# Window attention: the row maximum is taken off the scores by TensorE in PSUM instead of by VectorE

## The reference

```python
qkv = win @ w_qkv + b_qkv                        # win: (256 windows, 49, 32)
q, k, v = heads(qkv)                             # 4 heads, 8 channels each
attn = jnp.einsum('whnd,whmd->whnm', q, k) * scale
attn = jax.nn.softmax(attn, axis=-1)             # over the 49 keys m
out = jnp.einsum('whnm,whmd->whnd', attn, v)
out = out @ w_proj + b_proj
```

## Time and profile before

| | us |
|---|---|
| median of 3 runs | 478.54 |
| lowest, highest | 476.59, 478.87 |
| profiled execution | 475.85 |
| its span | 474.1 |
| VectorE busy in the span | 365.1 |
| TensorE matmul busy | 351.1 |
| ScalarE busy | 299.8 |
| GpSimd busy | 233.9 |
| first and last row-maximum reduction (start) | 31.8 and 141.6 |

### The profile page before, as it was taken

One profiled execution on the slowest core, in us unless ns is written; L12 is line 12 of the kernel. 1 busy time (PEld: TensorE's weight loads), 2 busy tenths in 40 slices (PEclk: granted clock), 3 DMA queues, 4 the chain that ended last, 5 costly groups with the idle time before them and its releaser, 6 DMA issues. The chain is left out here.

```text
span 474.1 us, 10021 instructions
## 1 busy us (share of the span) xinstructions
PE 351.1 (74%) x3480; PEld 230.4 (49%) x3480; DVE 365.1 (77%) x679; ACT 299.8 (63%) x583; POOL 233.9 (49%) x217
## 2 busy tenths in 40 slices
PE   5149888896789785985877647666795829888885
PEld 4037676675665332142233213222483519877774
DVE  3799999999797388799787999997576685544443
ACT  4327788887785899578758946347985253333432
POOL 4526868775673324966972999567081130000000
PEclk9997999998899999599897885768999668999999
DMA  6110000000223231022000000000030000111111
GB/s 147 5 18 3 3 1 0 0 1 0 59 60 70 51 87 29 1 60 58 1 0 1 0 1 0 0 0 1 3 68 3 1 0 11 20 19 22 22 19 24
DMA packets 24044, 10.29 MB, mean 22 GB/s; under 512 B 20576, under 2 KB 22368, under 8 KB 24016
## 3 DMA queue, kind: packets, MB, share of 16 engines
q1 hardware_dynamic: 23888, 9.93, 10.3%
q0 software_dynamic: 128, 0.01, 0.2%
HBM read 2.00 MB, written 1.61 MB: 8 GB/s over the span
## 5 line engine op out<-in xcount | busy, mean ns | idle before, releaser
L480 POOL TENSOR_TENSOR Pr<-Pr,rc 128x392 f32<-128x392 f32 x64 | 54.4, 883 | 32.2 <-DVE rc L1826 32.2
L511 POOL TENSOR_TENSOR YA<-YA,hC 128x784 f32<-128x784 f32 x27 | 51.7, 1914 | 32.4 <-DVE hC L1910 31.5
L1349 PE MATMUL pair<-BCf,sel 96*128 96x392 bf16 x128 | 38.4, 394 | 35.0 <-DVE Hs L1894 30.8
L1894 DVE TENSOR_TENSOR_SCAN Hs<-dA,pair 128x784 f32<-128x784 f32 x32 | 57.1, 1785 | 1.0
L1193 PE MATMUL pair<-ident,Pr 128*128 128x128 f32 x256 | 41.1, 293 | 13.2 <-ACT PT L715 9.0
L1349 PEld LDWEIGHTS pair<-BCf,sel 96*128 96x128 bf16 x128 | 10.2, 105 | 74.0 <-issue 71.6
L1193 PEld LDWEIGHTS pair<-ident,Pr 128*128 128x128 f32 x256 | 29.2, 146 | 25.1 <-ACT PT L715 15.8
L1887 DVE TENSOR_TENSOR pair<-DU,pair 128x784 f32<-128x784 f32 x32 | 31.1, 973 | 10.6 <-PE pair L1349 10.3
L715 ACT ACTIVATE PT<-pair 128x392 f32<-128x392 f32 x64 | 31.4, 497 | 5.9 <-PE pair L1193 5.6
L724 ACT ACTIVATE Pr<-Ts 128x392 f32<-128x392 f32 x64 | 32.5, 536 | 3.4 <-DVE Ts L1810 3.4
L1804 DVE TENSOR_REDUCE mx<-pair 128x8 f32<-128x392 f32 x64 | 32.6, 550 | 1.6 <-PE pair L1150 1.4
(11 more groups left out here) (262 smaller groups left out, 928.8 us busy)
## 6 DMA issues: line engine op xcount, KB each, us to landing
SX<-XP SPq DMA_DIRECT2D x48, 112.2 KB
XT<-in_x SPq DMA_DIRECT2D x4, 392.0 KB, 5.0
out<-Os SPq DMA_DIRECT2D x28, 56.0 KB, 1.8
AD<-Aa SPq DMA_DIRECT2D x4, 196.0 KB
NB<-in_L_conv_x_proj_w SPq DMA_DIRECT2D x4, 3.0 KB
DW<-in_L_conv_dw SPq DMA_DIRECT2D x4, 1.1 KB
vec<-in_L_conv_b_qkv POOLq DMA_DIRECT2D x3, 0.5 KB, 5.8
W<-in_L_conv_w_qkv SPq DMA_DIRECT2D x1, 48.0 KB
```

The lines of the kernel that those rows point to most:

```text
L480: eng.tensor_tensor(pg, pg, bcast(rc[:, g, :], 2, WT), ALU.mult).then_inc(pn_r, 1)
L511: eng.tensor_tensor(y, y, hC[:, n % NHC, :], ALU.add).then_inc(g_ya, 1)
L1349: ins = eng.matmul(SPREAD[s][:, columns(h)], sel[:, n, :], upper(BCf[:, c % 2, s, columns(h)]), start=True, stop=True)
L1894: eng.tensor_tensor_scan(Hs[:, n % 2, :], dA[:, n % NA, :], SPREAD[0], 0.0, ALU.mult, ALU.add).then_inc(v_s, 1)
```

## The change

The maximum is no longer subtracted by VectorE. For two groups at a time (a part), VectorE writes the 16 maxima of a partition as two bfloat16 pieces, an upper one (L1848) and the remainder (L1852), into `MP`. TensorE turns them against the identity into 32 rows of bank 7 (`turn_max`, L1175 of the changed kernel), and VectorE copies these to SBUF as `MT` in bfloat16 (L1857). TensorE then adds minus the maximum to the scores in their banks, with a matmul against a constant pattern `msel` (`shift`, L1183). The exponent reads PSUM. GpSimd sets `MT`, `mrow` and `msel` up at the start. `scores` now waits for the exponentials of the step before where it had waited for its subtractions. ScalarE's order changes too.

```diff
@@ TensorE, pe_att
-                        eng.wait_ge(sub_r, 4 * s - 2 + 2 * part)
+                        eng.wait_ge(exp_r, 4 * s - 2 + 2 * part)
...
-                                                 start=True, stop=True)
+                                                 start=pair == 0, stop=False, skip_group_check=True)
...
+                def turn_max(part):
+                    if not cur:
+                        return
+                    eng.wait_ge(max_r, 10 * s + (5, 8)[part])
+                    if part == 0 and (not fixed or s >= 2):
+                        eng.wait_ge(ao_r, s - 1)
+                    eng.matmul(shift_rows(part), MP[:, part, :], upper(ident[:, 0:QP]), start=True, stop=True,
+                               skip_group_check=True).then_inc(mt_r, 1)
+
+                def shift(part):
+                    if not cur:
+                        return
+                    eng.wait_ge(max_r, 10 * s + 9 + part)
+                    for g in (2 * part, 2 * part + 1):
+                        eng.matmul(banks[g][:, 0:392], MT[:, part, :], msel[:, g % 2].rearrange("p m k -> p (m k)"),
+                                   start=False, stop=True, skip_group_check=True).then_inc(sh_r, 1)
...
                 if prv:
                     transposes(0)
                     transposes(1)
+                turn_max(0)
                 if early:
                     early()
                 if prv:
                     transposes(2)
+                shift(0)
+                turn_max(1)
+                if prv:
                     transposes(3)
+                shift(1)
                 if prv2:
                     project()
@@ ScalarE, act_att
-                    eng.activation(Pr[:, par, g, :, 0:WT], Ts[:, g, :, :], ACT.Exp).then_inc(exp_r, 1)
+                    eng.activation(Pr[:, par, g, :, 0:WT], banks[g][:, 0:392].rearrange("p (m k) -> p m k", k=WT), ACT.Exp).then_inc(exp_r, 1)
 
                 turned_out(0)
+                turned_out(1)
+                turned_out(2)
                 exponent(0)
-                turned_out(1)
+                turned_out(3)
                 exponent(1)
-                turned_out(2)
-                turned_out(3)
                 exponent(2)
                 exponent(3)
@@ VectorE, dve_att
-                        for g in groups:
-                            eng.wait_ge(max_r, 4 * s + g + 1)
-                            if not fixed or s >= 1:
-                                eng.wait_ge(exp_r, 4 * (s - 1) + g + 1)
-                            eng.tensor_tensor(Ts[:, g, :, :], banks[g][:, 0:392].rearrange("p (m k) -> p m k", k=WT),
-                                              bcast(mx[:, g, :], 2, WT), ALU.subtract).then_inc(sub_r, 1)
...
+                    def upper_piece(part):
+                        eng.wait_ge(max_r, 10 * s + (2, 6)[part])
+                        if not fixed or s >= 1:
+                            eng.wait_ge(mt_r, 2 * s - 1 + part)
+                        eng.tensor_copy(MP[:, part, 0:16], mx[:, 2 * part:2 * part + 2, :].rearrange("p g m -> p (g m)")).then_inc(max_r, 1)
+
+                    def lower_piece(part):
+                        eng.wait_ge(max_r, 10 * s + (3, 7)[part])
+                        eng.tensor_tensor(MP[:, part, 16:32], mx[:, 2 * part:2 * part + 2, :].rearrange("p g m -> p (g m)"),
+                                          MP[:, part, 0:16], ALU.subtract).then_inc(max_r, 1)
+
+                    def turned_max(part):
+                        eng.wait_ge(mt_r, 2 * s + part + 1)
+                        eng.tensor_copy(MT[:, part, 0:QP], shift_rows(part)).then_inc(max_r, 1)
```

More of the change, by code:

```diff
@@ L113, in build @@
         Vst = sb("Vst", [P, 2, 2, NW // 2, G, 2, C], att)
-        Ts = sb("Ts", [P, G, 8, WT], att)
+        MP = sb("MP", [P, 2, 32], att, BF16)
+        MT = sb("MT", [32, 2, P], att, BF16)
+        mrow = sb("mrow", [32, 16], att)
+        msel = sb("msel", [32, 2, 8, WT], att, BF16)
         Pr = sb("Pr", [P, 2, G, 8, WP], att)
@@ L210, in build @@
         qk_d, v_r, s_r, t_r, av_r, pj_r, q_r, k_r, exp_r, ring_r = sems("qk_d v_r s_r t_r av_r pj_r q_r k_r exp_r ring_r")
-        xw_r, km_r, pn_r, max_r, sub_r, sum_r, rec_r, ao_r, x1_r = sems("xw_r km_r pn_r max_r sub_r sum_r rec_r ao_r x1_r")
+        xw_r, km_r, pn_r, max_r, mt_r, sh_r, sum_r, rec_r, ao_r, x1_r = sems("xw_r km_r pn_r max_r mt_r sh_r sum_r rec_r ao_r x1_r")
         PRODUCTS = "conv x2 u z delta xB xC out var wout".split()
@@ L236, in build, with shift_rows @@
         block = ctx.enter_context(nc.Block())
+        QP = 64 + WT
+        def shift_rows(part):
+            return banks[7][0:32, 256 + P * part:256 + P * part + QP]
         def strip(s):
@@ L457, in _ @@
                 eng.memset(m[:], 0.0).then_inc(s_mk2, 1)
+            eng.memset(MT[:], 0.0).then_inc(s_mk2, 1)
+            eng.wait_ge(s_mk, 5)
+            eng.tensor_tensor(mrow[:, :], ident[0:32, 0:16], ident[0:32, 16:32], ALU.add).then_inc(s_mk2, 1)
+            eng.wait_ge(s_mk2, 6)
+            eng.tensor_scalar(msel[:, :, :, :].rearrange("p g m k -> p (g m) k"), bcast(mrow[:, :], 2, WT), -1.0, None, ALU.mult).then_inc(s_mk2, 1)
             eng.wait_ge(s_mk2, 1)
@@ L720, in exponent @@
                         return
-                    eng.wait_ge(sub_r, 4 * s + g + 1)
+                    eng.wait_ge(sh_r, 4 * s + g + 1)
                     if not fixed or s >= 2:
                         eng.wait_ge(t_r, 4 * (s - 2) + g + 1)
-                    eng.activation(Pr[:, par, g, :, 0:WT], Ts[:, g, :, :], ACT.Exp).then_inc(exp_r, 1)
+                    eng.activation(Pr[:, par, g, :, 0:WT], banks[g][:, 0:392].rearrange("p (m k) -> p m k", k=WT), ACT.Exp).then_inc(exp_r, 1)
                 turned_out(0)
+                turned_out(1)
+                turned_out(2)
                 exponent(0)
-                turned_out(1)
+                turned_out(3)
                 exponent(1)
-                turned_out(2)
-                turned_out(3)
                 exponent(2)
@@ L1198, in av @@
                     eng.wait_ge(ring_r, base + G)
+                    if cur:
+                        eng.wait_ge(max_r, 10 * s + 10)
                     if not fixed or s >= 2:
@@ L1241, in _ @@
             pe_att(-1, 1)
+            eng.wait_ge(s_mk2, 7)
             for s in (0, 1, 2):
@@ L1283, in conv @@
                 if b == 0 and h == 0:
-                    eng.wait_ge(sub_r, 4 * NS - 2)
+                    eng.wait_ge(exp_r, 4 * NS - 2)
                 for y in taps:
@@ L1308, in delta @@
                 if b == 0:
-                    eng.wait_ge(sub_r, 4 * NS)
+                    eng.wait_ge(exp_r, 4 * NS)
                 eng.matmul(result("delta", b)[:, h, :], BD[:, U_DL, :], US[:, b, HT * h:HT * h + HT], start=True, stop=True).then_inc(p_["delta"], 1)
@@ L1799, in dve_att, with largest @@
                 if cur:
-                    for part in range(2):
-                        groups = (2 * part, 2 * part + 1)
-                        eng.wait_ge(s_r, 2 * s + part + 1)
-                        for g in groups:
-                            eng.tensor_reduce(mx[:, g, :], banks[g][:, 0:392].rearrange("p (m k) -> p m k", k=WT), AX.X,
-                                              ALU.max).then_inc(max_r, 1)
-                        for g in groups:
-                            eng.wait_ge(max_r, 4 * s + g + 1)
-                            if not fixed or s >= 1:
-                                eng.wait_ge(exp_r, 4 * (s - 1) + g + 1)
-                            eng.tensor_tensor(Ts[:, g, :, :], banks[g][:, 0:392].rearrange("p (m k) -> p m k", k=WT),
-                                              bcast(mx[:, g, :], 2, WT), ALU.subtract).then_inc(sub_r, 1)
+                    def largest(g):
+                        if g % 2 == 0:
+                            eng.wait_ge(s_r, 2 * s + g // 2 + 1)
+                        eng.tensor_reduce(mx[:, g, :], banks[g][:, 0:392].rearrange("p (m k) -> p m k", k=WT), AX.X,
+                                          ALU.max).then_inc(max_r, 1)
@@ new lines, in turned_max @@
+                    def turned_max(part):
+                        eng.wait_ge(mt_r, 2 * s + part + 1)
+                        eng.tensor_copy(MT[:, part, 0:QP], shift_rows(part)).then_inc(max_r, 1)
+                    largest(0)
+                    largest(1)
+                    upper_piece(0)
+                    largest(2)
+                    lower_piece(0)
+                    largest(3)
+                    upper_piece(1)
+                    lower_piece(1)
+                    turned_max(0)
@@ L1812, in dve_att @@
+                    turned_max(1)
                 if prv2:
```

## The result

The changed kernel takes 530.31 us (median of 5 runs, 529.92 to 534.85), the kernel before in the same comparison 476.59 (470.71 to 478.87). The ratio is 1.1215, with a 95% interval of 1.1116 to 1.1313. The sign of the forecast was right, but the size was not: +54 us where it said +16, and the time lies outside its range. The profiled execution took 534.85 us with a span of 533.1, against 475.85 and 474.1 before, so the differences of the two traces add up to 59.

The account below looks back on a forecast made before the run. VectorE's instruction list was taken to bound each attention step; 16 steps at +1.0 us, less 0.5 us, took 475.85 to 491.3, put at 492.5 us for the median of runs. Range 480 to 505, the forecast's own 487 to 501.

Parts of the forecast that it names:

- What bounds the kernel: Attention steps, 60 to 105 us: a step is as long as VectorE's list, 6.67 us; TensorE has some 0.7 us of room.
- What the change takes from VectorE: Four subtractions a step at 0.48 us spacing, 1.9 us; after added work and dependence gaps VectorE gains 0.85 us.
- What it adds to VectorE: Four 16-element pieces and two 113-element copies a step: 0.7 us of work, bounds 0.4 and 1.5, plus three gaps of 0.12.
- +8: Upper end of the range over 16 steps if VectorE's small instructions cost their upper bound, 0.5 us a step more.
- What it adds to TensorE: Two turnings and four shifts a step, 0.84 us, in a queue which had 0.7 us of room.
- The waits: VectorE waits 0.74 us before the second MT copy and 1.15 before the residual; step 7.6 us, taken as +1.0.
- What costs nothing: Exponentials reading PSUM cost ScalarE nothing; GpSimd's set-up falls into its 2.61 us wait, uncovered 0 to 2 us once.
- 0.5 us off for ScalarE's order: Stretch from 105 to 127 us: ring copies no longer stand behind exponentials, 0 to -3 us, taken as -0.5.
- VectorE's queue alone decides: TensorE answers in time, step 6.3 us, time 470 to 472, or 455 by the skill's prices; chance 0.09.
- Balance: Waits are served earlier as TensorE works ahead: +0.1 to +0.4 us a step, 477 to 483 us; chance 0.12.
- The clock rival: TensorE falls to its lower clock more often, some 1.8 us a step in half the steps: +14, 506 us; chance 0.12.
- a sign of being wrong: The forecast is wrong if the granted clock from 60 to 105 us isn't 1.00.

Follow-up runs that it names:

- the rebuilt kernel: Changed kernel with row maxima in PSUM and a new order on VectorE, TensorE (projection ahead of last shifts) and ScalarE: 488.81 us, 1.0278 of the kernel before.

## Why the prediction was wrong in size

**What bounds the kernel: right.** VectorE's list set the step: it was busy for 43.47 of 45 us, and cutting TensorE's work in the kernel before left the time where it was.

**What the change takes from VectorE: nearly.** With the maxima in PSUM, no piece held up, VectorE's busy time in the whole trace falls from 365.1 to 353.9 us, 0.7 us a step, where the forecast had 0.85 less work. From the first maximum to the first `MT` copy it is 2.74 us (71.85 to 74.59), laid out as 2.60.

**What it adds to VectorE: the step that failed.** I wrote "For 16 elements I take 0.17 long and 0.09 apart", with an upper bound of "each as long as the reciprocal's 0.25". Alone a piece does last 0.17. Measured in place it is 0.53 in the mean and 1.39 at most, because it stands still while GpSimd works. The nearest rows were small instructions without GpSimd beside them, and the reciprocal, which has it beside it, isn't stopped by it: all 32 stay within 240 and 254 ns after. I chose neighbours by size and not by where operands lie. That term was worth 31 of the 54 us: 23 inside the pieces, and 8 in what hangs on them. For TensorE waits for the pieces, its granted clock falls to 0.77, and its answers come later: VectorE's idle time from the first maximum to the last is 51.6 us in the changed kernel and 42.7 with the maxima in PSUM. The range of the sum had +8 for it.

**What it adds to TensorE: nearly.** A shift lasts 335 ns as priced (336), and a turning 225. But a pair of shifts takes 0.43 us of the queue and not 0.34, a turning 0.16 and not 0.08, and the quartet of transposes behind it 0.59 and not 0.53. TensorE's timeline, maxima in PSUM:

```profile
74.90 0.50 PE L1183 MATMUL pair<-msel,MT 32*128 32x392 bf16 x2 [0.25 <-DVE MT L1857]
75.33 0.23 PE L1175 MATMUL pair<-ident,MP 128*32 128x113 bf16 x1
75.49 0.66 PE L1223 MATMUL pair<-ident,Pr 128*128 128x128 f32 x4
76.08 0.50 PE L1183 MATMUL pair<-msel,MT 32*128 32x392 bf16 x2
76.51 0.60 PE L1205 MATMUL pair<-AO,BD 128*128 128x196 f32 x2
```

**The waits: right in place, a little small.** From the second turning's start to the projection's it is 1.18 us (75.33 to 76.51) where I laid out 0.95, and from there to the residual 0.77 instead of 0.64. These 0.36 us give the 0.27 between 1.42 and 1.15: I counted a copy's slot as 0.18, and the profile counts its whole 0.27 as work. The first upper piece starts 1.17 us after its first maximum (73.02 against 71.85) where I had 1.06, the first pair of shifts takes its 0.09 more ahead of the second turning, and the loop's branch leaves 0.56 us ahead of the maxima instead of 0.40, every other step. 7.6 + 0.36 + 0.11 + 0.09 + 0.08 is 8.24, and 8.0 to 8.4 was measured. The first ten of the 15 spacings of steps lose 1.45 us each (8.14 against 6.69), not 1.0. The last five, with the statistics and the table loads, lose 1.8 each (9.95 against 8.11). There I had taken 0.5 us off for ScalarE's order, and its gain in the kernel before isn't seen here; why isn't shown.

**What costs nothing: right.** The exponentials from PSUM have a median of 507 ns, where those from SBUF had a mean of 538. Set-up on GpSimd leaves the first maximum at 31.8 us, and the `MT` copies last 264 (0.28 forecast).

**The rivals.** That VectorE's queue alone decides was wrong, in the rebuilt kernel too, since TensorE takes over. Balance, at 477 to 483 us, didn't come either. The clock rival saw the fall (1.00 to 0.77), which the forecast had named as a sign of being wrong, and priced it at 14 us, where the runs leave 4.5 to 11. The fall follows from TensorE's waits for the pieces: with the maxima in PSUM the clock is 0.96. It isn't the main loss.

**The sum of +54:** 31 for the wait for GpSimd and the clock that falls with it, 9 to 12 for the residual behind the projection, and the remaining 11 to 14 for TensorE's added matmuls and the chain through the turnings. How this last part splits wasn't separated. The forecast's +16 was for the last two parts together, which measure 22; for the first it had nothing but the +8 of its range.

## What to carry to other kernels

Before a small instruction is priced by its size, look where its operands lie and what GpSimd does at that time: on VectorE, a cast of 16 elements from SBUF and a subtraction with two SBUF sources each took up to 1.4 us, nearly the whole of a GpSimd instruction of 1.5. The sign in a trace is a group whose maximum is many times its minimum and whose long members end just behind GpSimd's; a source in PSUM took it away here. And work taken off the bounding engine pays only up to the next one's room: here 0.7 us a step on TensorE, into which four shifts and two turnings (2 x 0.43 + 2 x 0.16 = 1.2 us) did not fit.

## What of the hardware was not expected

- Casts of 16 elements took 174 to 1425 ns by what GpSimd did; with the source in PSUM 173 to 176. So a cast of 0.17 us cost up to eight times that.
- The reverse was seen once: GpSimd's four products took 4.62 us instead of 3.27 beside VectorE's large casts.
- Reciprocals (128x16 from SBUF to SBUF, 236 to 255 ns) were never held up by GpSimd, though in the changed kernel 16 of 32 lie wholly within a GpSimd instruction.
- A granted clock of 0.77 instead of 1.00 from 60 to 105 us cost 4.5 to 11 us of 530. Twelve spare matmuls a step brought it back to 1.00, and took part of that again for themselves.
